# The first scan table built on POOL in place of DVE

## The reference

```
xn = layernorm(x)
x  = x + attn0(xn) + ffn0(xn)          # layer 0
xn = layernorm(x)
x  = x + attn1(xn) + ffn1(xn)          # layer 1

ffn0(xn):  hidden = silu(xn @ gate.T * gate_s) * (xn @ up.T * up_s)   # codes -1, 0, 1; 1792 wide
           hidden @ down.T * down_s

attn0(xn): h = xn @ Win.T + bin                                        # 64 wide
           4 times:
               y = silu(layernorm(h)*w + b)
               y = real(conv of y with p^t, plus last_conv * p^(t+1))  # p: one complex number a channel
               h = h + y * scl
               y = silu((layernorm(h)*w + b) @ W1.T + b1) @ W2.T + b2
               h = h + y
           layernorm(h) @ Wout.T + bout
```

## Time and profile before

| | before |
|---|---|
| median of 3 runs | 272.54 us (272.51 to 272.75) |
| the profiled execution, its own time | 272.88 us |
| its span in the profile | 270.8 us |
| PE busy | 264.0 us |
| DVE busy | 188.3 us |
| POOL busy | 149.1 us |
| ACT busy | 129.9 us |
| granted TensorE clock | 1.00 |

### The profile page before, as it was taken

One profiled execution on the slowest core, in us unless ns is written; L12 is line 12 of the kernel. 1 busy time (PEld: TensorE's weight loads), 2 busy tenths in 40 slices (PEclk: granted clock), 3 DMA queues, 4 the chain that ended last, 5 costly groups with the idle time before them and its releaser, 6 DMA issues.

```text
span 270.8 us, 4709 instructions
## 1 busy us (share of the span) xinstructions
PE 264.0 (98%) x1691; PEld 138.5 (51%) x1691; DVE 188.3 (70%) x300; ACT 129.9 (48%) x224; POOL 149.1 (55%) x182
## 2 busy tenths in 40 slices
PE   8899899999999999999999999999999999999995
PEld 3685545555554555555455554564444445444444
DVE  4799897787766787586955747899696667424313
ACT  2737474575564246674666654050176403355600
POOL 3878865566921201428555448353779793046680
DMA  6996999311100000201210000012310001200004
GB/s 240 330 238 178 262 213 224 65 41 35 43 2 1 2 0 7 73 0 39 53 43 0 2 1 2 0 46 69 101 49 0 0 4 49 101 7 0 0 2 155
DMA packets 12070, 18.14 MB, mean 67 GB/s; under 512 B 912, under 2 KB 6544, under 8 KB 12048
## 3 DMA queue, kind: packets, MB, share of 16 engines
q1 hardware_dynamic: 6912, 12.75, 15.0%
q0 software_dynamic: 4704, 4.72, 10.5%
q10 hardware_dynamic: 432, 0.38, 0.4%
HBM read 20.46 MB, written 2.10 MB: 83 GB/s over the span
## 4 chain that ended last, share of the span: by engine, by line
PE 84%; POOL 7%; DVE 5%; issue 2%; DMA 1%; ACT 0%; DVEq 0%; POOLq 0%
PE bank L756 18%; PE bank L639 14%; PE bank L640 14%; PE bank L607 9%; PE bank L609 9%; PE bank L608 9%; PE bank L687 3%; PE bank L718 2%; POOL root L1221 1%; PE bank L601 1%; PE bank L707 1%; PE bank L708 1%; DMA X<-in_x 1%; POOL prod L1258 1%; DVE xl L1015 1%
## 5 line engine op out<-in xcount | busy, mean ns | idle before, releaser
L1317 POOL TENSOR_TENSOR hidl<-hid,hidh 128x512 f16<-128x512 f32 x28 | 32.5, 1164 | 42.1 <-ACT hidh L825 41.8
L639 PE MATMUL bank<-xh,gatew 128*128 128x512 f16 (+1 forms) x136 | 43.9, 342 | 2.1 <-DVE hid L1151 1.3
L639 PE MATMUL bank<-xh,upw 128*128 128x512 f16 (+1 forms) x136 | 43.9, 341 | 0.0
L640 PE MATMUL bank<-xl,gatew 128*128 128x512 f16 (+1 forms) x136 | 43.8, 341 | 0.0
L640 PE MATMUL bank<-xl,upw 128*128 128x512 f16 (+1 forms) x136 | 43.8, 341 | 0.0
L756 PE MATMUL bank<-downw,hidh 128*128 128x512 f16 x112 | 42.5, 379 | 0.0
L756 PE MATMUL bank<-downw,hidl 128*128 128x512 f16 x112 | 42.4, 379 | 0.0
L1221 POOL TENSOR_TENSOR root<-var,powers 128x4 f32<-128x4 f32 (+1 forms) x25 | 24.0, 964 | 30.8 <-DVE var L1062 29.2
L1323 POOL TENSOR_TENSOR actl<-hid,acth 128x512 f16<-128x512 f32 (+1 forms) x22 | 25.6, 1172 | 22.5 <-ACT acth L832 22.4
L920 ACT ACTIVATE silu<-bank,early 128x512 f32<-128x512 f32 x28 | 19.3, 688 | 26.1 <-PE bank L640 24.4
L1183 DVE SCALAR_TENSOR_TENSOR hid<-bank,early,silu 128x512 f32<-128x512 f32 (+1 forms) x22 | 16.5, 751 | 18.5 <-ACT silu L935 17.9
(11 more groups left out here) (183 smaller groups left out, 563.8 us busy)
## 6 DMA issues: line engine op xcount, KB each, us to landing
X<-in_x SPq DMA_DIRECT2D x7, 256.0 KB, 7.5
downw<-in_down POOLq DMA_DIRECT2D x2, 896.0 KB, 15.2
out_x<-X SPq DMA_DIRECT2D x7, 256.0 KB, 2.0
stage<-in_v SPq DMA_DIRECT2D x6, 256.0 KB, 2.7
stage<-in_mask SPq DMA_DIRECT2D x4, 256.0 KB, 8.5
stage<-in_weight SPq DMA_DIRECT2D x4, 256.0 KB, 2.6
gatew<-in_gate POOLq DMA_DIRECT2D x1, 896.0 KB, 14.6
upw<-in_up POOLq DMA_DIRECT2D x1, 896.0 KB, 12.7
```

The lines of the kernel that those rows point to most:

```text
L639: pe.matmul(bank_of(key)[:, c], w, xh[b][:, k, c], start=(k == 0), stop=False)
L640: mm = pe.matmul(bank_of(key)[:, c], w, xl[b][:, k, c], start=False, stop=(k == KT - 1))
L1317: pool.tensor_tensor(hidl[:, n % FT, :], hid[:, n % UNITS, :], hidh[:, n % FT, :], ALU.subtract).then_inc(hid_lo, 1)
```

## The change

POOL builds table 0 too, at the same place of the step list, with the same three instructions as the other tables. DVE's part of the step is gone. `rot_t` loses the half that DVE used. The count `table_ready` now covers all four tables, so the scan of layer l of the first half waits for l + 1, also for l = 0, where DVE had its own table in order.

```diff
-        r4 = overlay(mini + [("rot", DEPTH * SEQ, F32), ("rot_t", 2 * SEQ, F32),
+        r4 = overlay(mini + [("rot", DEPTH * SEQ, F32), ("rot_t", SEQ, F32),
...
-        rot_t = r4["rot_t"][:].rearrange("p (a t) -> p a t", a=2)
+        rot_t = r4["rot_t"][:]
...
-        def outer(eng, l, part, work):
+        def outer(eng, l, part):
...
-            tmp_ = rot_t[:, work, :].rearrange("p (a c) -> p a c", a=ROOTN)
+            tmp_ = rot_t.rearrange("p (a c) -> p a c", a=ROOTN)
...
-                elif kind == "table" and step[1] == 0:
-                    dve.wait_ge(tables_ready, 1)
-                    for part in range(3):
-                        emit(outer(dve, 0, part, 0), hold=part > 0)
...
                     if l == 0:
                         dve.wait_ge(rad_ready, 1)
-                    elif b == 0:
-                        dve.wait_ge(table_ready, l)
+                    if b == 0:
+                        dve.wait_ge(table_ready, l + 1)
...
-                elif kind == "table" and step[1] > 0:
+                elif kind == "table":
                     for part in range(2):
-                        link(outer(pool, step[1], part, 1))
-                    outer(pool, step[1], 2, 1).then_inc(table_ready, 1)
-                    pool.wait_ge(table_ready, step[1])
+                        link(outer(pool, step[1], part))
+                    outer(pool, step[1], 2).then_inc(table_ready, 1)
+                    pool.wait_ge(table_ready, step[1] + 1)
```

## The result

The changed kernel took 273.50 us in the median of 10 runs (273.31 to 275.19), the kernel before 272.55 us (272.24 to 272.87). By the medians that is 0.95 us, or 0.35%, slower. The measured ratio is 1.0054, 95% interval [1.0043, 1.0065]; it is the higher because it weighs all ten runs (their mean is 274.1 us), and they lie in two groups. The profiled execution took 273.44 us with a span of 271.6.

What follows compares the result with a forecast made beforehand. PE's full stream from 38 us bounds the kernel, so the t1 transposes' start decides; POOL's queue, table included, moves it from 37.36 to 38.37: 272.54 + 1.01 = 273.55 us, range 273.0 to 274.2, chance 0.83.

Steps and rivals of the forecast that it cites:

- The place: Start of the four t1 transposes on PE (L687): starting them x us later ends the run x us later.
- The gain: Without DVE's table, `hid` of unit 3 runs earlier and PE's gate tile of unit 5 starts 1.45 us sooner.
- The loss: POOL's table stands in front of the root that releases the t1 transposes; they start at 38.37, 1.01 us later.
- the pair of `hidl`: POOL's second and third `hidl`: 2.33 us, 0.04 less for the next start; from 30.80 to POOL free at 33.09.
- the table: Table 0 on POOL, between the third `hidl` and that of unit 3: 2.21 us, links between instructions included.
- the `hidl`: POOL's `hidl` of unit 3, behind the table: 1.11 us from its start to the root behind it.
- the root with its way to `lno`: Inverse root of the first mini-norm on POOL, 1.02 us, then 0.10 from its end to `lno` on DVE.
- `lno` to t1: From the start of `lno` on DVE to the t1 transposes on PE: 0.84 us.
- The choice of the short pair: POOL's second and third `hidl` take 2.33 us, not 2.48, with no DVE table beside them.
- The faster rival: POOL covers the table before the root; transposes at 35.59, 1.77 us earlier, 270.8 us; turning point 1.20 us; chance 0.05.
- The clock: PE's clock falls in the new 2.78 us gap before t1: up to 2.96 us more, 276.5; chance 0.04.
- a sign that the prediction itself named as one of being wrong: On PE behind the gap before t1: matmuls running 0.43 apart would show the prediction wrong.

Runs made afterwards that it cites:

- with two tables: Edit of the changed kernel: POOL builds table 0 twice in a row, with the same result; 278.02 us, ratio 1.0197 to the kernel before.
- the four versions: Kernels with 0, 1.41, 2.20 and 4.41 us of table on POOL in front of the root; 271.27, 272.73, 273.50 and 278.02 us.
- the version with 1.41 us: Edit of the changed kernel: POOL does only the two products of table 0, DVE does the sum; 272.73 us, ratio 1.0000.
- The six runs again: The changed kernel measured once more without an edit, on the chip of three single executions; median 275.02 us.

## Why the prediction was right, and what it gave too little weight

**The place.** It said that the start of the t1 transposes stands for the whole run. It does. From the start of t1 to the end of the span it is 233.4 us in the kernel before (270.8 - 37.36) and in the changed one (271.6 - 38.24), and between 233.4 and 233.5 in every other profiled execution whose clock held behind t1, with one exception: the version with the table late on DVE, which met a second condition at z, has 234.2. Where the clock fell behind t1 it is 235.1 twice and, with two tables, 235.7.

**The gain.** `hid` of unit 3 was put at 28.9 and is at 28.86. The gate tile was put at 31.67 and is at 31.93, without a gap; PE came to it 0.26 us later because its stream in this execution was that much behind from an earlier place (the transposes at 31.49, not 31.23). That hides behind the next gap and changed nothing.

**The loss.** From the start of the second `hidl` to t1 the sum gave 38.37 - 30.80 = 7.57 us; it is 7.54. The terms: the pair of `hidl` 2.29 predicted, 2.24 measured; the table 2.21 and 2.20; the `hidl` 1.11 and 1.11; the root with its way to `lno` 1.12, and 37.40 - 36.25 = 1.15; `lno` to t1 0.84 and 0.84. The choice of the short pair, and the rule of the Trainium skill behind it (page "SBUF — State Buffer", section "SBUF: two separate sides"), is borne out: the pair is 2.28 long, not 2.48, and the table on DVE away from POOL takes under a third of its time. A third sign lies in the version with the table behind the root, where the W1 part on DVE (L1109, two SBUF inputs) ran beside POOL's table and took 1.09 us in place of 0.69.

**The faster rival.** Its turning point was put at 1.20 us of table; the line of the four versions gives 1.22, and the version with 1.41 us came out at 1.0000 [0.9992, 1.0009]. With no table in front it predicted 271.3, and 271.27 was measured. Its mechanism was right and its condition isn't met by the change, as the prediction said.

**The clock.** This is where the prediction was off. It gave the fall of PE's clock in the new gap 0.04 and a price of up to 2.96 us. Of the 19 executions of the changed kernel, ten took 274.8 us or more. In the two of them that a profile caught, the clock fell within a microsecond of the gap's end; with the gap filled by matmuls, seven of seven stayed on the shorter level. So the rival comes about as often as the forecast, at a price near 1.6 us, not 2.96. The forecast of 273.55 fits the shorter level (273.31 to 273.55), while the mean over all executions is nearer 274.3. That the median of the first ten runs was 273.50 is in part luck: six of the ten were on the shorter level. The six runs again have a median of 275.02, and all 19 executions one of 274.81, both outside the forecast's 273.0 to 274.2. And a sign that the prediction itself named as one of being wrong, matmuls 0.43 apart behind the gap, is there in the two profiled executions of the longer level. The step that failed is the sentence "against it: PE is busy on both sides of the gap": that is no reason. The price was taken from the first matmuls of the run, where the slow pace lasted longer (and is read from the pace alone: the granted clock reads 1.00 there). Behind the gap it was seven or eight matmuls at 0.43 in place of 0.22, so about 0.21 each, and a part of what stood beside them. The Trainium skill's rule (page "TensorE: Matmul & The Clock Gate", section "Part 1: The HAM clock gate") spoke for this rival, and the traces now agree with its direction. The page has the rise of the clock at the start come at a time that differs from run to run; that a fall behind a gap can come in one run and not in the next is what the runs here show.

What stays open is what decides, in a single execution, whether the clock falls: gaps of 2.55 and 2.64 us were seen with the fall and one of 2.57 without it, so in this range the length alone doesn't decide. A mean clock of 0.994 or below was seen now and then elsewhere too, in two of 22 executions of the kernel before (273.05 and 273.86 us), at a place no profile shows.

## What to carry to other kernels

Moving work off an engine that is late is half of a change; the other half is what stands behind it in the queue of the engine that gets it. Here three instructions two tasks earlier or later on the same engine are the difference between 0.95 us lost and 1.3 us won, and the list of what is queued behind them told which. Where one engine's stream is full from some point on, follow that engine's last gap back and count everything in microseconds at that point. And a gap on PE can cost more than its length: here one of 2.6 us cost a further 1.6 in about half of the executions and one of 4.7 us a further 2.4, while the profile of the kernel before shows no fall behind its gap of 1.3 us. Keep such a gap short, or fill it with matmuls into a bank that is free anyway.

## What the hardware showed that I had not expected

- Ten of 19 executions of the changed kernel took 1.6 us longer at a mean clock of 0.994; both that were profiled show TensorE at 1.2 GHz behind a gap of 2.6 us. With a gap of 4.7 us all four executions had a clock below 1.000 (one profiled), at 2.4 us of time. Seven executions whose gap was filled with 2.2 us of constant matmuls had a clock of 0.999 or more, and took no longer.
- The clock can fall at 9 to 14 us too; in the one profiled execution of the changed kernel that shows it, it cost nothing, since a later wait took it up.
- A DVE instruction with two SBUF inputs of 256 floats took 0.42 to 0.43 us with POOL idle, and 1.38 to 1.77 us beside POOL's `hidl` and weight loads. Which of the two does it is plain only for POOL's arithmetic: the instruction of 1.38 us had weight loads beside it, but the W1 part (two SBUF inputs of 512 floats), which has one beside it in the kernel before and in the changed one, took 0.69 us there as elsewhere.
